# Weight-staging stores for h2 and w3 issued from SyncE instead of ScalarE

## The reference

```python
x = _layernorm(x + conv(x, filt))
h = silu(x @ w1.T * s1) * (x @ w2.T * s2)       # 1024 -> 4096
h = gelu(h @ h1.T * sh1)                        # 4096 -> 4096
h = gelu(h @ h2.T * sh2)                        # 4096 -> 4096
x = _layernorm(x + h @ w3.T * s3)               # 4096 -> 1024
```

## Time and profile before

| what | value |
|---|---|
| median of 3 runs | 3873.06 us (3871.66 to 3890.75) |
| the profiled execution's own time | 3874.94 us |
| its span on core 6 | 3873.4 us |
| spans of the 8 cores | 3844.7 to 3873.4 us |
| TensorE busy | 2876.1 us (74%) |
| VectorE busy | 722.9 us (19%) |
| ScalarE busy | 296.5 us (8%) |
| GpSimd busy | 490.3 us (13%) |
| first quarter's h1 stage | 1209 to 1593 us |

### The profile page before, as it was taken

One profiled execution on the slowest core, in us unless ns is written; L12 is line 12 of the kernel. 1 busy time (PEld: TensorE's weight loads), 2 busy tenths in 40 slices (PEclk: granted clock), 3 DMA queues, 4 the chain that ended last, 5 costly groups with the idle time before them and its releaser, 6 DMA issues.

```text
span 3873.4 us, 39143 instructions; the slowest of 8 cores (3844.7 to 3873.4 us)
## 1 busy us (share of the span) xinstructions
PE 2876.1 (74%) x13920; PEld 1379.9 (36%) x13920; DVE 722.9 (19%) x1397; ACT 296.5 (8%) x461; POOL 490.3 (13%) x890
## 2 busy tenths in 40 slices
PE   0624344353167556999699999969999978999995
PEld 0212111121033222445444444634444453444445
DVE  5333333333312221000310000041000022000003
ACT  0000000000011000000110000011000002100000
POOL 2333333343301322000000000000000000000000
PEclk9867676676588778999899999989999999999987
DMA  7878787787857997444444444534434444443432
GB/s 205 226 199 247 226 260 230 233 263 225 241 163 231 298 279 250 152 152 152 134 160 152 152 152 152 171 129 154 153 147 154 152 158 144 158 153 147 153 130 84
DMA packets 321265, 709.01 MB, mean 183 GB/s; under 512 B 72800, under 2 KB 236704, under 8 KB 294448
## 3 DMA queue, kind: packets, MB, share of 16 engines
q1 hardware_dynamic: 139520, 423.68, 30.9%
q0 software_dynamic: 80176, 207.28, 18.7%
q10 hardware_dynamic: 101376, 75.54, 6.6%
HBM read 588.91 MB, written 113.25 MB: 181 GB/s over the span
## 4 chain that ended last, share of the span: by engine, by line
PE 59%; DMA 22%; DVE 7%; issue 3%; ACTq 2%; POOL 2%; SPq 1%; DVEq 1%; ACT 1%; POOLq 0%
PE ps L166 56%; DMA h2s<-wstgb 6%; DMA wstgf<-h 5%; DMA wstgf<-w 4%; DMA h1s<-wstgb 4%; PE ps L164 3%; ACTq L248 2%; DMA w3s<-wstgb 2%; POOL x1bf L361 2%; DVE wstgb L238 1%; DMA xstg<-x 1%; SPq L248 1%; DVEq L60 1%; DVE stats L288 1%; DVE sqs L289 1%
## 5 line engine op out<-in xcount | busy, mean ns | idle before, releaser
L166 PE MATMUL ps<-gT,hsl 128*128 128x512 bf16 x3968 | 900.1, 386 | 142.8 <-ACT uT L467 138.3
L166 PE MATMUL ps<-uT,hsl 128*128 128x512 bf16 x3968 | 891.3, 383 | 4.3 <-ACT uT L467 4.3
L166 PE MATMUL ps<-xwh,Fh 128*128 128x512 bf16 x544 | 226.9, 417 | 593.0 <-DVE xwl L275 593.0
L166 PEld LDWEIGHTS ps<-gT,hsl 128*128 128x128 bf16 x3968 | 392.4, 99 | 632.0 <-issue 180.4
L166 PE MATMUL ps<-x1T,wsl 128*128 128x512 bf16 x1792 | 436.2, 384 | 213.1 <-DMA wsl<-w2s 114.2
L166 PEld LDWEIGHTS ps<-uT,hsl 128*128 128x128 bf16 x3968 | 391.3, 99 | 484.0 <-issue 52.0
L238 DVE CAST wstgb<-wstgf 128x512 bf16<-128x512 f32 x704 | 303.0, 430 | 727.1 <-DMA wstgf<-h 243.7
L525 DVE TENSOR_TENSOR y<-ps,s3bt 128x256 f32<-128x256 f32 x64 | 27.2, 425 | 1848.7 <-PE ps L164 1848.7
L233 POOL DMA_DIRECT2D wstgf<-h x512 | 287.8, 566 | 545.8 <-DVE wstgb L238 489.0
L166 PEld LDWEIGHTS ps<-x1T,wsl 128*128 128x128 bf16 x1792 | 176.8, 99 | 430.2 <-issue 224.4
L536 POOL DMA_DIRECT2D tmpf<-x1f x16 | 8.7, 543 | 2323.6 <-DVE y L541 1922.4
(11 more groups left out here) (52 smaller groups left out, 712.3 us busy)
## 6 DMA issues: line engine op xcount, KB each, us to landing
wstgf<-h POOLq DMA_DIRECT2D x512, 256.0 KB, 5.2
hsl<-h1s SPq DMA_DIRECT2D x64, 2048.0 KB, 8.0
hsl<-h2s SPq DMA_DIRECT2D x64, 2048.0 KB, 7.8
wstgf<-w POOLq DMA_DIRECT2D x192, 256.0 KB, 6.1
h1s<-wstgb SPq DMA_DIRECT2D x512, 64.0 KB, 4.3
h2s<-wstgb ACTq DMA_DIRECT2D x512, 64.0 KB, 4.6
wsl<-w1s SPq DMA_DIRECT2D x32, 1024.0 KB, 5.6
wsl<-w2s SPq DMA_DIRECT2D x32, 1024.0 KB, 6.9
```

The lines of the kernel that those rows point to most:

```text
L166: sc.run("tensor", lambda t, a=lt, b=rh, o=out_ap, s=st: t.matmul(o, a, b, start=s, stop=False))
```

## The change

The stores of the h2 and w3 cast jobs are put on SyncE's list, where those of w1, w2 and h1 already are. The number, size and order of the stores stays the same, and so do all events that others wait for.

```diff
     cast_weight("w1", w1_h, w1s, D, HID, 512)
     cast_weight("w2", w2_h, w2s, D, HID, 512)
     cast_weight("h1", h1_h, h1s, HID, HID, 256)
-    cast_weight("h2", h2_h, h2s, HID, HID, 256, wq="scalar")
-    cast_weight("w3", w3_h, w3s, HID, D, 256, wq="scalar")
+    cast_weight("h2", h2_h, h2s, HID, HID, 256)
+    cast_weight("w3", w3_h, w3s, HID, D, 256)
```

## The result

The changed kernel takes 3896.0 us (median of 34 runs) against 3877.1 us (37 runs of the kernel before); the ratio is 1.0045, with an interval of 1.0027 to 1.0063. That is 17 us slower (10 to 24), where 24 us and 3897 us were predicted. The likeliest case came true, but its size, 0.45%, lies just inside "within 0.5%" (chance 0.30) and not in "slower by over 0.5%" (0.64).

The account below looks back on a forecast made before the run. The prediction took the h1 stage as bound by the chain load, cast, store on nearly full DMA engines. Stage end + 22, Tc (last cast store issued) + 2 and convolution 0 gave + 24 us, median 3897 us, range 3877 to 3922.

Parts of the forecast that it names:

- The likeliest case: Whole kernel: Tc gains up to 3 us or loses up to 15; 3892 to 3912 us, likeliest 3897, chance 0.58.
- What bounds the stage: h1 stage, 175 cast jobs: the chain load, cast, store on nearly full DMA engines limits, 312 us; TensorE keeps up.
- The late block: Behind the last cast store: block 10's load is issued only then, so the stage ends 22 us later (20.7 to 26.3).
- Tc: h1 stage: time at which the last cast store has been issued; claimed 2 us later, ends 21 earlier and 34 later.
- rival B: h1 stage: the shared queue stops the casts for the whole of each h1 load; 56 us, 3929 us, chance 0.12.
- Rival A: h1 stage: stores freed from Gelu operations tighten the cast chain, paying for the late block; middle 3884 us, chance 0.24.
- The convolution: Convolution tiles: 290 stores move from ScalarE to SyncE; 0 us taken, ends 0 and 3 us gained.
- The sum: Whole kernel: stage end + 22, Tc + 2, convolution 0, together + 24 us; median 3897 us.
- C: End of the h1 stage: nothing changes, as block 10's load could pass the stores; its chance is counted in Rival A.
- D: Whole kernel: faster by over 19 us, for which Tc would have to come 41 us earlier; chance 0.06.

Follow-up runs that it names:

- e3: The changed kernel with each first-quarter h1 load ahead of its cast group's stores on SyncE; ratio 1.0025 to the kernel before.
- e4: The changed kernel with each first-quarter h1 load two cast groups earlier on SyncE; ratio 0.9991 to the kernel before.
- e1: The kernel before with only the convolution's h2 stores moved to SyncE, those of the h1 stage left on ScalarE; ratio 1.0004.
- e7: The changed kernel with 7 instead of 16 cast jobs per h1 block and each h1 load two cast groups earlier; 3775.9 and 3787.3 us.
- e2: The kernel before with only the stores of the first quarter's h1 stage (175 cast jobs) moved to SyncE; ratio 1.0050.

## Why the prediction was right, step by step

**What bounds the stage.** Right: the last cast store sets the end of the h1 stage, and behind it TensorE runs blocks bare. e3 and e4 move the number of bare blocks by one each and the time by 14.1 and 13.1 us.

**The late block, + 22 us.** Measured 21.9 us over eight cores (24.2 between the two slowest). Its parts on core 3: the load of block 10 was waited for until 10.2 us after the last store (9.3 taken), and block 10 took 16.6 us (15.3 taken), its first 31 matmuls 9.60 us instead of 8.35, after 10.29 us of idling instead of 5.27. Block 9 ended 0.1 us before the last store, within the 1 us before to 8 us after that was worked out. From its load's issue to its end block 9 took 28.1 us (27.5 taken, 28.4 allowed), so the ten blocks ahead did stay hidden, but with hardly anything to spare. Block 0 started 12.7 us after its load was issued, where some 10 were named.

**Does Tc move, + 2 us.** Measured - 1.3 us over eight cores, within the spread of single cores (308 to 316 us in both). The ends of - 21 and + 34 were far too wide. What the reasoning named is partly visible: the load in the rows above stops the casts for 11.5 us instead of 8.8 (rival B's mechanism), 0.6 us more in the mean of 80 loads, but the loads of the next five jobs have landed meanwhile, and five casts run back to back. Rival A's gain, stores freed from the Gelu operations, can't be seen by itself. That the two sides cancel is argued, not shown by a run of its own: that the sum came out near nothing is shown, and the + 2 was in part luck.

The rule of the Trainium skill on turns between rings ("DMA: Bandwidth & Descriptors", "Queues, rings and completion order") was taken as rival B's end in the prediction; the trace shows no such cost. Landing of the h2 stores with their own queue was 1.6 to 15.2 us, on the shared one it is 1.5 to 14.3 us (median 5.3 instead of 5.2). The other section of that page of the Trainium skill, "Issuing engines are not separate DMA queues", says that issuing from several engines saves only issue time. For the cast stream the runs agree with it: 315.0 and 310.4 us from first to last cast in e3 and e4, against 312.3, and the same convolution in e1. The 21.9 us behind the stream come from what stands behind what on SyncE's list.

**The convolution, 0.** Right (e1).

**The sum.** 24 us predicted, 17 us timed (10 to 24), 20.6 us from the first cast to the first h2 matmul. The 3.3 us between 24 and 20.6 are Tc; 20.6 lies within the interval of the timed runs. Two small slips change nothing: the cast jobs of this stage have 350 stores, not 348, and a loss of up to 15 us on top of 22 ends at 3910, not 3912.

**Rivals.** A and B are excluded by the first column of the tables (311.0 us against the 291 and 346 of their full size), C by SyncE's timeline and the 21.9 us, D by the result.

## What to carry to other kernels

A DMA is an instruction in its engine's list: putting a paced stream of stores ahead of a prefetch turns the prefetch into a load on demand, and at the end of the stream that costs one load and one block: 22 us here. Count what is left to run behind the last item of the stream: here 72 us were left in the kernel before, and spreading the stream over all blocks (7 jobs per block instead of 16) was worth 3.4%, against 0.45% for the engine that issues it. Where streams are spread, every prefetch beside them has to be looked at, that of the next stage too: the one that e7 left behind the stores cost 16 us.

## What was not expected of the hardware

With one queue fewer at work, the DMA engines were busy less: 89.0 MB took 93.2% of 311 us, 89.6 MB now 89.8% of 312 us, yet the casts went no faster. It is no matter of one core. Between first and last cast the mean share of eight cores is 0.933 in the kernel before and in e1, where ScalarE issues the stores of this stretch, and 0.904 to 0.909 in the changed kernel, e2, e3 and e4, where SyncE does. Some of it is work: in that stretch the kernel before moves 90.7 MB and the changed one 89.5, 1.3% less in 0.4% less time (means of eight cores). What the rest is stays open.

So the busy share fell and the pace stayed: a share of 0.93 with five buffers was not the engines' limit, and the 21 us of idle time were no gain to be had by issuing the stores from SyncE. Eight buffers got 14 of them, at a share of 0.976.
